# Softmax attention on one core: the value product as a 512-wide and a 256-wide matmul, row sums from GpSimd

## The reference

```python
h = relu(layernorm(x))                 # x: 4096 x 256
q, k, v = h @ Wq.T + bq, h @ Wk.T + bk, h @ Wv.T + bv
a = q @ k.T / 16 + adj + adj           # adj: 4096 x 4096
out = x + softmax(a, axis=-1) @ v
```

## Time and profile before

| | |
|---|---|
| median of 3 runs | 814.09 us (814.0 to 814.21) |
| the profiled execution | 813.88 us, of which the span of the trace is 812.1 us |
| TensorE busy | 804.5 us, 99% of the span |
| VectorE, ScalarE, GpSimd busy | 588.9 us (73%), 361.1 us (44%), 383.5 us (47%) |
| granted TensorE clock | full in all slices of the page |

### The profile page before, as it was taken

One profiled execution on the slowest core, in us unless ns is written; L12 is line 12 of the kernel. 1 busy time (PEld: TensorE's weight loads), 2 busy tenths in 40 slices (PEclk: granted clock), 3 DMA queues, 4 the chain that ended last, 5 costly groups with the idle time before them and its releaser, 6 DMA issues.

```text
span 812.1 us, 16621 instructions
## 1 busy us (share of the span) xinstructions
PE 804.5 (99%) x6708; PEld 802.7 (99%) x6708; DVE 588.9 (73%) x982; ACT 361.1 (44%) x651; POOL 383.5 (47%) x333
## 2 busy tenths in 40 slices
PE   8999999999999999999999999999999999999998
PEld 8999999999999999999999999999999999999998
DVE  6868777776777777777777767777776777777754
ACT  6683443334344434444443444444344434444365
POOL 4546736072633708264280825527082551718273
PEclk9999999999999999999999999999999999999999
DMA  8521333243333324333333333323333332333200
GB/s 263 183 80 54 117 91 111 73 131 92 92 111 89 114 79 123 99 89 108 92 106 91 108 101 92 118 80 112 96 104 106 91 109 77 115 104 93 91 27 14
DMA packets 43996, 81.68 MB, mean 101 GB/s; under 512 B 5008, under 2 KB 5904, under 8 KB 43920
## 3 DMA queue, kind: packets, MB, share of 16 engines
q1 hardware_dynamic: 43344, 79.84, 33.1%
q10 hardware_dynamic: 576, 0.79, 0.3%
HBM read 76.42 MB, written 4.19 MB: 99 GB/s over the span
## 4 chain that ended last, share of the span: by engine, by line
PE 96%; DVE 1%; ACT 1%; POOL 1%; issue 0%; POOLq 0%; DVEq 0%
PE ps L335 49%; PE ps L437 15%; PE ps L439 15%; PE ps L438 15%; PE ps L327 1%; PE ps L316 1%; PE ps L412 0%; PE ps L419 0%; ACT x_pair L515 0%; POOL v L289 0%; DVE x_third L618 0%; PE ps L346 0%; POOL rstd L275 0%; ACT v_full L533 0%; ACT hT L505 0%
## 5 line engine op out<-in xcount | busy, mean ns | idle before, releaser
L335 PE MATMUL ps<-qhl,hT 128*128 128x256 f32 x3072 | 405.9, 282 | 0.0
L335 PEld LDWEIGHTS ps<-qhl,hT 128*128 128x128 f32 x3072 | 383.5, 189 | 0.0
L306 POOL TENSOR_TENSOR ring_a<-ring_a,m_row 128x512 f32<-128x512 f32 x179 | 230.1, 1320 | 210.4 <-ACT m_row L584 210.4
L437 PE MATMUL ps<-v,p_hi 128*128 128x258 f32 x1024 | 291.8, 285 | 0.3 <-DVE p_lo L675 0.3
L439 PE MATMUL ps<-v,p_lo 128*128 128x258 f32 x1024 | 289.4, 283 | 0.0
L438 PE MATMUL ps<-v,p_hi 128*128 128x256 f32 x1024 | 289.1, 282 | 0.0
L580 ACT CAST p_hi<-ps 128x512 fp32r<-128x512 f32 x256 | 150.5, 588 | 245.7 <-PE ps L439 243.7
L641 DVE TENSOR_TENSOR ring_a<-ps,ring_a 128x512 f32<-128x512 f32 x179 | 123.4, 689 | 101.5 <-PE ps L335 100.5
L437 PEld LDWEIGHTS ps<-v,p_hi 128*128 128x128 f32 x1024 | 194.1, 190 | 0.5 <-DVE p_lo L675 0.5
L439 PEld LDWEIGHTS ps<-v,p_lo 128*128 128x128 f32 x1024 | 194.2, 190 | 0.0
L438 PEld LDWEIGHTS ps<-v,p_hi 128*128 128x128 f32 x1024 | 193.1, 189 | 0.0
(11 more groups left out here) (76 smaller groups left out, 358.7 us busy)
## 6 DMA issues: line engine op xcount, KB each, us to landing
ring_a<-in_adj SPq DMA_DIRECT2D x179, 256.0 KB, 2.6
ring_b<-in_adj SPq DMA_DIRECT2D x77, 256.0 KB, 2.7
x_res<-in_x SPq DMA_DIRECT2D x16, 256.0 KB, 3.0
out<-x_res SPq DMA_DIRECT2D x15, 256.0 KB, 2.0
x_pair<-in_x SPq DMA_DIRECT2D x5, 512.0 KB, 4.5
x_third<-in_x SPq DMA_DIRECT2D x2, 512.0 KB, 4.6
w_all<-in_w ACTq DMA_DIRECT2D x3, 256.0 KB, 4.1
x_pair<-in_x SPq DMA_DIRECT2D x4, 128.0 KB, 2.8
```

Of the source, the lines that this page charges most:

```text
L306: nc.gpsimd.tensor_tensor(slot_tiles(w), slot_tiles(w), m, ALU.subtract).then_inc(s_sub, 1)
L335: last = nc.tensor.matmul(dst, lhs(a, ib), rhs(c, ib), start=(n == 0), stop=(n == 3 * DB - 1))
L437: nc.tensor.matmul(ps[:, at, 0:VW], hi, v[:, n, 0:VW], start=(n == 0), stop=False)
```

## The change

- `v` is stored as v_hi and v_lo side by side, 512 columns. p_hi multiplies both in one 512-wide matmul (a whole PSUM bank); p_lo multiplies v_hi in a 256-wide one. An output bank then holds two partial results, which `finish` adds one after the other.
- The columns of ones are gone. The row sums of blocks 0 to 14 are made by GpSimd: ScalarE computes the exponential of a slot a second time, in place, and GpSimd adds the slot to `sums`. Units 6 and 11 of a block (`JOINED`) have no second exponential: VectorE adds their PSUM exponential to the slot before. The last block's sums are added up by VectorE from PSUM, each behind its `write_p_lo`.
- VectorE joins the two halves of `sums` (`join_sums`), TensorE turns them (`turn_sums`, two transposes in the middle of a block's last `weigh_values`), VectorE reduces them and takes the reciprocal (`reduce_sums`).
- ScalarE copies a block's first logits to the PSUM bank of the running maximum (`seed_max`); a block's last `running_max` is three half-size operations.
- `LAG` is 21, the ring has 24 slots, and a slot is loaded again when it has been summed. `turn_max` stands behind the values of its step, not ahead. Where a new block of values begins, the scores of two steps stand ahead of it.
- `m_row` has one buffer in place of two.

```diff
-    LAG = UNITS + 6
+    LAG = UNITS + 5
+    JOINED = (6, 11)
+    SUM_UNITS = tuple(u for u in range(1, UNITS) if u + 1 not in JOINED)
...
-    RING = 23
+    RING = 24
...
-        v = sb("v", [P, TILES, D + VW], f32r)
+        v = sb("v", [P, TILES, 2 * D], f32r)
...
+        def to_gpsimd(w):
+            return w // UNITS < BLOCKS - 1
...
-                if s >= RING:
-                    sp.wait_ge(s_exp, s - RING + 1)
+                w = s - RING
+                if w >= 0 and w % UNITS in JOINED:
+                    sp.wait_ge(s_exp, w + 1)
+                elif w >= 0:
+                    sp.wait_ge(s_sum, sum_count(w if w % UNITS in SUM_UNITS else w + 1))
...
+            def sum_slot(w):
+                b, u = w // UNITS, w % UNITS
+                if u == 1:
+                    if b > 0:
+                        pool.wait_ge(s_scols, b)
+                    pool.wait_ge(s_exp2, w + 1 - pair_count(w))
+                    nc.gpsimd.tensor_tensor(sums[:, :], slot(w - 1), slot(w), ALU.add).then_inc(s_sum, 1)
+                    return
+                if u in JOINED:
+                    pool.wait_ge(s_pair, pair_count(w))
+                else:
+                    pool.wait_ge(s_exp2, w + 1 - pair_count(w))
+                pool.wait_ge(s_sum, sum_count(w) - 1)
+                nc.gpsimd.tensor_tensor(sums[:, :], sums[:, :], slot(w - 1 if u in JOINED else w), ALU.add)\
+                    .then_inc(s_sum, 1)
+
+            def sums_due(w):
+                b, u = w // UNITS, w % UNITS
+                if u == UNITS - 1:
+                    return (w - 3, w - 2)
+                if u == 1:
+                    return (w - 3, w - 2)
+                if u in (0, 2):
+                    return ()
+                return (w - 3,)
...
+                subtract_max(w)
+                for n in sums_due(w):
+                    if n >= 0 and n % UNITS in SUM_UNITS and to_gpsimd(n):
+                        sum_slot(n)
...
+            def turn_sums(b):
+                pe.wait_ge(s_scols, b + 1)
+                pe.wait_ge(s_m, min(b + 2, BLOCKS))
+                for i in range(QS):
+                    last = nc.tensor.transpose(ps[:, X_BANK, i * P:(i + 1) * P], max_rows[:, i, :], ident[:, :])
+                last.then_inc(s_sturn, 1)
...
-                elif u == 0 and b > 0:
-                    pe.wait_ge(s_fin, b)
                 pe.wait_ge(s_plo, w + 1)
                 for i in range(QS):
+                    if u == 0 and 0 < b < BLOCKS - 1:
+                        pe.wait_ge((s_fin0, s_fin)[i], b)
                     for k in range(KT):
                         n = KT * u + k
                         hi = p_hi[:, w % PB, k, i * P:(i + 1) * P]
                         lo = p_lo[:, w % PB, k, i * P:(i + 1) * P]
                         at = o_bank(b) + i
-                        nc.tensor.matmul(ps[:, at, 0:VW], hi, v[:, n, 0:VW], start=(n == 0), stop=False)
-                        nc.tensor.matmul(ps[:, at, 0:D], hi, v[:, n, VW:VW + D], start=False, stop=False)
-                        last = nc.tensor.matmul(ps[:, at, 0:VW], lo, v[:, n, 0:VW], start=False,
-                                                stop=(n == TILES - 1))
-                    if w == STEPS - 1 and i == 0:
-                        last.then_inc(s_half, 1)
+                        if n < TILES - 1:
+                            nc.tensor.matmul(ps[:, at, :], hi, v[:, n, :], start=(n == 0), stop=False)
+                        last = nc.tensor.matmul(ps[:, at, 0:D], lo, v[:, n, 0:D], start=False, stop=False)
+                    if u == UNITS - 1:
+                        last = nc.tensor.matmul(ps[:, at, :], hi, v[:, n, :], start=False, stop=True)
+                    if u == UNITS - 1 and i == 0:
+                        last.then_inc(s_pv0, 1)
+                        turn_sums(b)
...
+            def opens_block(s):
+                return s not in HOLD and due(s) > 0 and due(s) % UNITS == 0
+
             for s in range(FIRST, STEPS + LAG + len(HOLD)):
                 b, u = s // UNITS, s % UNITS
-                if s < STEPS:
+                if s < STEPS and not opens_block(s - 1):
                     scores(s)
+                if s + 1 < STEPS and opens_block(s):
+                    scores(s + 1)
                 if s == FIRST:
                     project_v(GROUPS - 1, 1)
-                if u == 0 and b <= BLOCKS:
-                    turn_max(b - 1)
                 if u == 1 and b <= BLOCKS:
                     spread_max(b - 1)
                 if u == UNITS // 2 and b + 1 < BLOCKS:
                     project_q(b + 1)
                 if s not in HOLD and due(s) >= 0:
                     weigh_values(due(s))
+                if u == 0 and b <= BLOCKS:
+                    turn_max(b - 1)
...
+                if w >= 2 and ((w - 2) % UNITS in JOINED or not to_gpsimd(w - 2)):
+                    act.wait_ge(s_pair, pair_count(w - 2) if to_gpsimd(w - 2) else direct_count(w - 2))
                 nc.scalar.activation(ps[:, E_BANK + w % 2, :], slot(w), ACT.Exp, scale=2.0).then_inc(s_exp, 1)
+                if to_gpsimd(w) and w % UNITS not in JOINED:
+                    act.wait_ge(s_exp, w + 1)
+                    nc.scalar.activation(slot(w), slot(w), ACT.Exp, scale=2.0).then_inc(s_exp2, 1)
...
+            def seed_max(b):
+                act.wait_ge(s_add, UNITS * b + 1)
+                act.wait_ge(s_cols, b)
+                nc.scalar.copy(ps[:, A_BANK, :], slot(UNITS * b)).then_inc(s_seed, 1)
...
+                rows_max = max_rows[:, :, :]
+                nc.vector.tensor_tensor(rows_max, kept_half[:, 0], new_half[:, 0], ALU.max).then_inc(s_acc, 1)
+                dve.wait_ge(s_acc, 2 * b + 1)
+                nc.vector.tensor_tensor(rows_max, kept_half[:, 1], rows_max, ALU.max).then_inc(s_acc, 1)
+                dve.wait_ge(s_acc, 2 * b + 2)
+                nc.vector.tensor_tensor(rows_max, rows_max, new_half[:, 1], ALU.max).then_inc(s_cols, 1)
...
+                if not to_gpsimd(w):
+                    sum_directly(w)
+                elif w % UNITS in JOINED:
+                    dve.wait_ge(s_exp2, w - pair_count(w) + 1)
+                    nc.vector.tensor_tensor(slot(w - 1), ps[:, E_BANK + w % 2, :], slot(w - 1), ALU.add)\
+                        .then_inc(s_pair, 1)
+
+            def sum_directly(w):
+                e = ps[:, E_BANK + w % 2, :]
+                if w % UNITS == 0:
+                    dve.wait_ge(s_scols, BLOCKS - 1)
+                    nc.vector.tensor_copy(sums[:, :], e).then_inc(s_pair, 1)
+                else:
+                    dve.wait_ge(s_pair, direct_count(w) - 1)
+                    nc.vector.tensor_tensor(sums[:, :], e, sums[:, :], ALU.add).then_inc(s_pair, 1)
+
+            def join_sums(b):
+                if b < BLOCKS - 1:
+                    dve.wait_ge(s_sum, sum_count(UNITS * b + UNITS - 1))
+                    dve.wait_ge(s_bcast, b + 2)
+                else:
+                    dve.wait_ge(s_pair, direct_count(STEPS - 1))
+                    dve.wait_ge(s_sturn, b)
+                halves = sums[:, :].rearrange("p (k i n) -> p k i n", k=KT, i=QS)
+                nc.vector.tensor_tensor(max_rows[:, :, :], halves[:, 0], halves[:, 1], ALU.add).then_inc(s_scols, 1)
+
+            def reduce_sums(b):
+                dve.wait_ge(s_sturn, b + 1)
+                nc.vector.tensor_reduce(out=row_sum[:, :],
...
+                dve.wait_ge(s_sred, b + 1)
+                nc.vector.reciprocal(inv_sum[:, :], row_sum[:, :]).then_inc(s_inv, 1)
 
             def finish(b):
-                dve.wait_ge(s_pv, UNITS * (b + 1))
-                nc.vector.reciprocal(inv_sum[:, :], ps[:, O_BANK:O_BANK + QS, D]).then_inc(s_inv, 1)
                 dve.wait_ge(s_inv, b + 1)
                 dve.wait_ge(s_xb, b + 1)
                 for i in range(QS):
-                    last = nc.vector.scalar_tensor_tensor(x_res[:, i], ps[:, O_BANK + i, 0:D], inv_sum[:, i:i + 1],
-                                                          x_res[:, i], ALU.mult, ALU.add)
-                last.then_inc(s_fin, 1)
-
-            def finish_last():
-                dve.wait_ge(s_xb, BLOCKS)
-                for i in range(QS):
-                    dve.wait_ge((s_half, s_pv)[i], (1, STEPS)[i])
-                    at = o_bank(BLOCKS - 1) + i
-                    nc.vector.reciprocal(inv_sum[:, i:i + 1], ps[:, at, D:D + 1]).then_inc(s_inv, 1)
-                    dve.wait_ge(s_inv, BLOCKS + i)
-                    nc.vector.scalar_tensor_tensor(x_res[:, i], ps[:, at, 0:D], inv_sum[:, i:i + 1], x_res[:, i],
-                                                   ALU.mult, ALU.add).then_inc((s_last, s_fin)[i], 1)
+                    dve.wait_ge((s_pv0, s_pv)[i], (b + 1, UNITS * (b + 1))[i])
+                    for half in range(2):
+                        if half:
+                            dve.wait_ge(s_mid, QS * b + i + 1)
```

(14 more changed lines are left out.)

87 lines of the change are left out of this document (58 added, 29 removed).

## The result

| | before | after |
|---|---|---|
| median of the runs | 814.05 us | 825.55 us (4 runs, 824.45 to 827.63) |
| ratio | | 1.0143, 95% interval 1.013 to 1.0156 |
| span of the trace | 812.1 us | 823.0 us |

What follows compares the result with a forecast made beforehand. TensorE's dense stream, busy 99% of the span, was taken as the bound. 813.9 - 25.5 (pair) + 3.6 (turned sums) + 0.8 (maximum) + 4.4 (end) = 797.2 us, range 789 to 815.

Steps and rivals of the forecast that it cites:

- The pair: TensorE's value matmuls: 1024 triples of 360 ns become pairs of 335.1 ns, -25.5 us.
- rival B: Excess belongs to streaming 4-byte columns: a 512-wide matmul costs 239 ns, gain only 1.7 us, 821.0 us; chance 0.09.
- The 256-wide term: The pair's 256-wide value matmul on TensorE stays at 119.4 ns.
- The scores: TensorE's score matmuls, 119 ns each before; the sum held no term for a change in them.
- Turned sums: Two transposes on TensorE in each of 16 blocks, 32 x 0.113 = +3.6 us.
- Maximum: Between turn_max and spread_max TensorE waits some 0.05 us, 16 times: +0.8 us.
- keeps its lead: GpSimd with 195 added sums needs 2.56 us in a step of 2.77, so costs nothing on the path.
- The covers at a block's end: At the closing step, join ready before turn_sums by 0.3 us, next p_lo at 14.0, wanted at 14.3: thin but hold.
- rival C: A thin cover at the block's end breaks: 15 x 1.3 = +19.5 us, 816.7 us; chance 0.13.
- The end: Behind the last scores, waits for p_lo and the join plus additions behind the last matmul: +4.4 us.
- the p_lo behind `finish`: At the end, unit 241's p_lo stands behind VectorE's additions: ready 12.9, wanted 10.5, wait 2.4 us.
- the waits of 0.3, 0.35 and 0.35 us for p_lo: Behind the last scores, ScalarE's owed second exponentials for units 237 to 239 make TensorE's value units wait that long.

Runs made afterwards that it cites:

- e10: The changed kernel with row_sum declared behind x_res, so ring, p_hi and p_lo start 32 bytes lower: 822.6 us, ratio 1.01.
- e4_no_gpsimd_sums: The changed kernel without second exponentials, GpSimd's sums and VectorE's additions at joined units (row sums of blocks 0 to 14 left out): 817.31 us, ratio 1.004.
- e6_finish_late: The changed kernel with the last block but one's finish two p_lo later: 824.79 us, ratio 1.0132.
- e2_widths: The kernel before with only the pair, plus rows of twelve matmuls of each width behind the last values; executed once for its trace, no time given.
- e18: The changed kernel with an unused 32-byte tensor ahead of p_hi, moving p_hi, p_lo and x_res but not the ring: 820.56 us, ratio 1.008.
- e17: The kernel before with only the pair (row sums, low part left out), plus 32 unused bytes ahead of the ring: 811.28 us, ratio 0.9965.
- e14: The kernel before with 32 unused bytes ahead of the ring, moving ring, p_hi and p_lo: 814.51 us, ratio 1.0008.
- e15: The kernel before with 32 unused bytes ahead of p_hi, the ring staying in place: 814.83 us, ratio 1.001.
- e12: The kernel before with the pair, ones inside the 512 columns (last low column left out) and the last finish but one two p_lo later: 809.86 us.
- e16: The pair with ones inside the 512 columns and late finish, against before, plus ring, p_hi and p_lo 32 bytes higher: 809.33 us, ratio 0.9937.
- e5: The changed kernel with row_max and row_shift kept in PSUM: 823.67 us, ratio 1.0116.

## Why the prediction was wrong, by its own steps

- **The pair.** This is the step that failed first: "loading 128 columns of 4-byte weights takes about 0.11 us, runs under the matmul before, and a 256-wide matmul is just too short to hide it", and so 215.7 ns for 512 columns. The first part fits the floor of 0.112 us. The conclusion doesn't follow: the rows of narrow matmuls showed that there is a floor, not that 256 columns lie on it. The argument that the prediction held for rival B, "no fp32r row is under 119", was the better one, for 256 columns cost more than the floor. Measured 0.2335 us in the probe, 0.231 to 0.235 in the kernel; a triple was 362.6 ns in the mean (360 in the prediction) and the pair is 353.7, so the gain is 9.1 us, not 25.5. The 256-wide term (119) was right.
- **But the pair alone doesn't make the kernel slower.** With the measured gain the prediction's own sum is 813.9 - 9.1 + 3.6 + 0.8 + 4.4 = 813.6 us: no change, and still inside its range. The profiled execution took 824.8, 27.6 us more than predicted. Of these the pair makes 16.4, the scores 4.6, the end 4.3, the spread maxima 1.4, the start 0.5; the turned sums were 0.2 cheaper, and 0.6 has no place. So the sign was lost in steps that the prediction took as free or as small.
- **Rival B** had its deciding point at a pair of 351 ns and a 512-wide matmul of 232. The pair came out at 353.7, on the slower side of it, and it was given 0.09. Its 821.0 lies near the result in part by luck: it priced the pair 7.4 us too high, and the scores, the end and the spread maxima, 10.3 us together, made up for that and more.
- **The scores** were taken as unchanged, without a word. They cost +4.6 us through the placement of tensors, which the change shifts by the 32 bytes that the new `row_sum` takes (`e10` moves it and the sets are short again). Nothing in the trace of before could show this.
- **Turned sums**: 0.226 us a block predicted, 0.21 measured. Right.
- **Maximum**: 0.05 us a block predicted, 0.15 measured, with "but GpSimd idles then" as the reason for taking no port delay. GpSimd no longer idles there: it still makes sums of the block then, which the prediction counted for GpSimd but not beside this step. And the last of the 16 was taken like the others, with the 1.42 us of scores to cover it. It has no scores behind it: without GpSimd's sums it waits 1.2 us (`e4_no_gpsimd_sums`), with them 3.2.
- **GpSimd** "keeps its lead": it doesn't. It waits 30 times for VectorE's joined additions, 20 of them (73.4 us) in the row of the waits above. The prediction priced these additions on VectorE and didn't list who waits for them. In the middle this costs nothing; at the last block it puts a sum and a subtraction beside VectorE's work on the maximum, and the join behind a full row of GpSimd's work.
- **The covers at a block's end** (rival C) held: the join, which ended before `turn_sums` wanted it, shows in no wait of TensorE in the main part. Margins of 0.3 us were enough.
- **The end**: +4.4 us predicted, +8.7 measured (and the 0.6 without a place). More than predicted: the last maximum (3.2, where before waited 0.5), the eight pairs at half clock (2.3), and 1.3 in place of 0.3 behind the last matmul. Less: the p_lo behind `finish` (1.7 for 2.4), and the waits of 0.3, 0.35 and 0.35 us for p_lo, which don't show. That these don't show, and that the join has its 1.0 for 1.0, is luck: the half clock filled both. At full clock (`e6_finish_late`) three units there start 0.2 to 0.3 us late, 0.7 together, and the join waits 2.6.

So one step was costed from a mechanism in place of a bound, another was left out of the sum, and the last block was priced like those in the middle.

## What to carry to other kernels

When a change rests on the cost of an instruction shape that the trace does not show, a few dozen of that shape at the end of a program price it; a floor seen on narrow shapes says nothing on what sets the next wider one. Price the last block by itself: what covers a step in the middle is not there at the end. Work moved to an idle engine needs a list of who waits for it and for whom it waits, above all behind the last work of the bounding engine, where nothing covers it. When a stream that wasn't touched gets slower by 1 or 2%, shift the tensors by 32 bytes before looking for a cause in the schedule.

## What the runs showed of the hardware that was not expected

- TensorE streams fp32r at 0.45 to 0.46 ns a column at the full granted clock (256 columns 118 ns, 384 173, 512 233.5), bf16 at 0.42 (512 columns 216 ns); fp32r matmuls of 64 and 128 columns with weights of their own stand 112 ns apart (all in `e2_widths`).
- The place of operands in SBUF, by 32 bytes, changes TensorE's step: the changed kernel by 2.9 us (`e10`) and 5.0 us (`e18`), the pair alone by 3.5 (`e17`), the kernel before by at most 0.8 us (`e14`, `e15`), the kernels with the ones inside by nothing that can be told (`e12`, `e16`). The cause is open.
- While TensorE stood for 3.2 us in the kernel after, its granted clock fell to 0.50 (781:782 shows 0.82, 782:783 0.50); it was full again from some 788.5 us on. With the same stand of 3.2 us it stayed full in `e6_finish_late` and `e10_ring_8_bytes_lower`. So the length of a stand doesn't decide it alone, and the half clock cost 0.3 us where the work behind it waited for another engine anyway.
- A VectorE addition of two columns with its operands in SBUF took 0.99 us beside GpSimd's additions of 1.26 us, and 0.16 us without them (`e4`); with its operand in PSUM 0.17 (`e5`).
